# First attention of three fused transformer layers: when VectorE normalises the heads, and in which order TensorE and ScalarE take the neighbouring work

## The reference, cut to what matters

```
h = layer_norm(x, ln1_g, ln1_b)
q, k, v = split(h @ w_qkv.T)              # 16 heads of 16 features
scores = q_chunk . [k_previous_chunk, k_chunk] / 4      # chunks of 128 tokens
valid: the 128 keys that end with the query's own       # j >= i+1 and j <= i+128
attn = softmax(scores, -1);  out = attn @ [v_previous, v_chunk]
x = x + out @ w_o.T
x = x + mlp(layer_norm(x, ln2_g, ln2_b))  # 256 -> 1024 -> 256, gelu
```

## Time and profile before

| | |
|---|---|
| median of 3 runs | 1760.74 us |
| profiled execution, its own time | 1759.69 us |
| its span in the trace | 1757.9 us |
| granted TensorE clock, mean | 0.996 |
| PE busy / DVE / ACT / POOL | 1695.5 / 1446.6 / 1170.4 / 1052.0 us |
| reciprocals of attention A (one per chunk) | 32, from 40.0 to 371.2 us |

### The profile page before, as it was taken

The page is one execution under the profiler, slowest core; times in us unless marked ns, Lnnn a source line. Parts: engine busy times, 40 slices in busy tenths (PEclk is TensorE's granted clock), DMA queues, the critical chain, the costliest instruction groups (busy, mean ns, idle before and its releaser), DMA issues.

```text
span 1757.9 us, 43282 instructions
## 1 busy us (share of the span) xinstructions
PE 1695.5 (96%) x15168; PEld 1460.7 (83%) x15168; DVE 1446.6 (82%) x3686; ACT 1170.4 (67%) x3024; POOL 1052.0 (60%) x1052
## 2 busy tenths in 40 slices
PE   6999999989999999999998999999999999999997
PEld 4777777779998788888887888878888888888886
DVE  6888988868887999989997655579999999967776
ACT  6999888855544778878775343367787787743332
POOL 3676566534334687887774444367878777634333
PEclk9999999999999999999999999999999999999999
DMA  3111211022322322222223313122222222131221
GB/s 109 38 38 38 65 38 35 26 103 66 117 72 65 98 81 66 76 76 66 80 67 89 107 54 99 54 92 75 80 63 81 72 70 81 56 111 60 73 84 37
DMA packets 174626, 125.44 MB, mean 71 GB/s; under 512 B 20824, under 2 KB 173664, under 8 KB 173664
## 3 DMA queue, kind: packets, MB, share of 16 engines
q1 hardware_dynamic: 174432, 122.98, 23.0%
HBM read 88.32 MB, written 34.61 MB: 70 GB/s over the span
## 4 chain that ended last, share of the span: by engine, by line
PE 84%; DVE 9%; ACT 3%; issue 3%; DMA 1%; POOL 0%; SPq 0%; POOLq 0%; DVEq 0%; ACTq 0%
PE psum L612 18%; PE psum L614 17%; PE psum L613 17%; PE psum L948 6%; PE psum L916 5%; PE psum L929 5%; PE psum L727 3%; PE psum L709 3%; PE psum L890 3%; ACT a_probs L1757 2%; PE psum L662 1%; DVE a_neg_max L1240 1%; DVE psum L1238 1%; PE psum L699 1%; PE psum L1053 1%
## 5 line engine op out<-in xcount | busy, mean ns | idle before, releaser
L1876 ACT ACTIVATE b_probs<-masked,neg_max 128x256 f32<-128x256 f32 (+1 forms) x512 | 249.8, 489 | 119.4 <-DVE neg_max L1370 119.4
L612 PE MATMUL psum<-wa_hi,b_h_hi 128*128 128x512 f32 (+1 forms) x576 | 234.4, 407 | 6.0 <-DVE wa_lo L1167 3.6
L614 PE MATMUL psum<-wa_hi,b_h_lo 128*128 128x512 f32 (+1 forms) x576 | 214.1, 372 | 0.0
L613 PE MATMUL psum<-wa_lo,b_h_hi 128*128 128x512 f32 (+1 forms) x576 | 214.0, 372 | 0.0
L1370 DVE CUSTOM_DVE_ANT_0 masked<-psum,mask 128x256 f32<-128x256 f32 (+1 forms) x512 | 177.2, 412 | 41.1 <-PE psum L916 40.2
L612 PE MATMUL psum<-g_h_hi,wm_hi 128*128 128x512 f32 (+1 forms) x480 | 190.3, 397 | 3.5 <-POOL g_h_lo L2148 2.4
L2105 POOL TENSOR_TENSOR g_in<-g_in,minus_half 128x16 f32<-128x16 f32 x64 | 187.7, 2933 | 5.3
L614 PE MATMUL psum<-g_h_hi,wm_lo 128*128 128x512 f32 (+1 forms) x480 | 189.2, 394 | 0.0
L613 PE MATMUL psum<-g_h_lo,wm_hi 128*128 128x512 f32 (+1 forms) x480 | 189.2, 394 | 0.0
L1962 ACT ACTIVATE gate<-psum,vec_b 128x512 f32<-128x512 f32 x96 | 66.0, 687 | 153.6 <-PE psum L614 153.5
L612 PE MATMUL psum<-wm_hi,u_hi 128*128 128x256 f32 x576 | 164.5, 286 | 0.1
(11 more groups left out here) (167 smaller groups left out, 5432.6 us busy)
## 6 DMA issues: line engine op xcount, KB each, us to landing
b_inv_t<-inverse_rows SPq DMA_DIRECT2D x128, 128.0 KB, 3.0
x_mid<-y_out SPq DMA_DIRECT2D x96, 128.0 KB, 2.3
rope_in<-in_rope SPq DMA_DIRECT2D x64, 128.0 KB, 2.4
x_res<-x_state SPq DMA_DIRECT2D x64, 128.0 KB, 2.8
g_in<-x_mid SPq DMA_DIRECT2D x32, 256.0 KB, 3.7
w_raw<-in_w_mlp_b SPq DMA_DIRECT2D x2, 2154.0 KB, 9.1
x_in<-in_x SPq DMA_DIRECT2D x32, 128.0 KB, 2.2
x_res<-in_x SPq DMA_DIRECT2D x32, 128.0 KB, 2.2
```

The costliest lines, as they stand in the source:

```text
L612: nc.tensor.matmul(out, a_hi, b_hi, start=first, stop=False)
L613: nc.tensor.matmul(out, a_hi, b_lo, start=False, stop=False)
L614: return nc.tensor.matmul(out, a_lo, b_hi, start=False, stop=last)
L1876: ins = nc.scalar.activation(out, src, ACT.Exp, bias=neg_max[:, r, k:k + 1], scale=-1.0, accum_out=row_sum[:, n % 2, 4 * r + k:4 * r + k + 1])
```

## The change

Three orders are changed; no instruction is added or removed.

- VectorE: `normalize_heads` is split into `invert_heads` (the reciprocal, still first) and `normalize_heads` (the multiplication), which now comes behind `maxima(4s)` and ahead of `maxima(4s+1)`.
- TensorE: `project_qk(s+1)` moves ahead of `transpose_o(s-2)` and `transpose_z(s+2)`.
- ScalarE: `o_high(s-2)` moves behind `exponentials(4s)`.

```diff
@@ TensorE, pe_attention_a
                 if a_chunk(s - 1):
                     transpose_probs(4 * s - 1)
-                if a_chunk(s - 2) and s < NCH - 1:
-                    transpose_o(s - 2)
                 if s == NCH - 1:
...
                     pe_mlp(pe, MLP_A, MA, None, opening="z")
-                if s == -1:
-                    project_qk(0)
+                if a_chunk(s + 1):
+                    project_qk(s + 1)
+                if a_chunk(s - 2) and s < NCH - 1:
+                    transpose_o(s - 2)
                 if a_chunk(s + 2):
                     transpose_z(s + 2)
-                if a_chunk(s + 1) and s > -1:
-                    project_qk(s + 1)
                 if a_chunk(s):
                     transpose_probs(4 * s)
@@ VectorE, dve_attention_a
-            def normalize_heads(n):
+            def invert_heads(n):
                 v.wait_ge(S["out_steps"], a_out_step(n, 0))
                 src = bank[a_heads_bank(n)].rearrange("p (h d) -> p h d", d=32)
                 nc.vector.reciprocal(a_inv[:], src[:, :, 16]).then_inc(S["o_ready"], 1)
+
+            def normalize_heads(n):
+                src = bank[a_heads_bank(n)].rearrange("p (h d) -> p h d", d=32)
                 v.wait_ge(S["o_ready"], 2 * n + 1)
...
                 if a_chunk(s - 2) and s != NCH + 1:
+                    invert_heads(s - 2)
+                if a_chunk(s):
+                    maxima(4 * s)
+                if a_chunk(s - 2) and s != NCH + 1:
                     normalize_heads(s - 2)
                 if a_chunk(s):
-                    maxima(4 * s)
                     maxima(4 * s + 1)
...
                 elif s == NCH:
+                    invert_heads(NCH - 1)
                     normalize_heads(NCH - 1)
@@ ScalarE, act_attention_a
+                if a_chunk(s):
+                    exponentials(4 * s)
                 if a_chunk(s - 2) and s != NCH - 1:
                     o_high(s - 2)
-                if a_chunk(s):
-                    exponentials(4 * s)
                 if a_chunk(s + 1):
                     copy_twice(s + 1, 1)
```

## The result

The changed kernel takes 1772.15 us (median of 6 runs, 1766.77 to 1772.75) against 1760.58 us (6 runs, 1759.04 to 1761.61). By the medians it is slower by 11.6 us, where 6.1 us were forecast. The ratio estimated from the runs is 1.0054, with a 95% interval of 1.0043 to 1.0065; that is 9.5 us (7.6 to 11.4), less than the medians say. The six runs of the changed kernel lie at two levels, two at 1766.77 and 1768.62 us and four from 1772.07 to 1772.75. The median lies 0.65 us above the upper end of the forecast's range (1771.5). The sign and the path of the delay held; one term of the sum was too small, and about 2.5 us of the median lie outside the steps (an estimated 1.2 of them the clock in step 31).

The account below looks back on a forecast made before the run. TensorE, busy for 96%, was taken as the bound. 27 steps at 0.20 us (5.4) plus 0.28 (step 17), 0.33 (step 29) and 0.1 us (step 31) made 6.1 us, giving 1766.8 us, range 1759.5 to 1771.5.

Parts of the forecast that it names:

- the path of the delay: Second scores, heads, first scores, first maximum, first exponentials, `o_high`, k, second exponentials, second scores: 0.20 us shifts the whole step.
- First maximum: VectorE: moving the multiplication gains the step's first maximum 0.00 us, since the scores hold it.
- faster: Rival: the multiplication holds the first maximum, so 29 steps give back 8.4 us, 1752.3 us; chance 0.14.
- `o_high`'s place: ScalarE, between first exponentials and the copy of k: 0.28 us less 0.08 us of slack, 0.20 us a step.
- `transpose_o` "just in time": TensorE: the multiplication releases `transpose_o` at 214.88, it could begin near 214.89; `o_high` released at 215.54, when ScalarE reaches it.
- larger loss: Rival: VectorE's whole 0.33 us slip reaches the second scores in every step, 9.6 us, 1770.3 us; chance 0.12.
- the second maximum: VectorE: moves back by 0.33 us, to an end at 216.15, and no longer matters to the second exponentials.
- The range's lower end: Lower end of the forecast's own range, 1764.5 to 1769.5 us, given as 0.15 to 0.3 us a step.
- step 17: Fewer values matmuls and no slack before its second scores, so it loses 0.28 us.
- step 29: VectorE also carries the MLP's statistics and ScalarE waits for its maximum, so the full 0.33 us counts.
- Step 31: No `o_high` there; MLP transposes wait for heads about 1.7 us later, filling a 1.23 us gap: about 0.1 us.
- The gap: TensorE's idle before the transposes of a step's first probabilities, held by ScalarE's exponentials, stays at 0.29 us.

Follow-up runs that it names:

- gates by part: Kernel before, with each of a round's four transposes waiting for its own exponential instead of all four: 1759.55 us against 1762.80, ratio 0.9982.
- ScalarE's edit alone: Kernel before with only `o_high` moved behind the exponentials of round 4s: 1768.17 us, ratio 1.0027.
- without VectorE's: Changed kernel with the multiplication back before the step's first maximum, TensorE's and ScalarE's edits kept: 1766.93 us, ratio 1.0031.
- VectorE's edit alone: Kernel before with only the split of reciprocal and multiplication on VectorE: 1802.56 us against 1762.14, one run.
- the second trace: Changed kernel timed again with no edit: 1771.78 us against 1762.80, ratio 1.0050.
- trace 3: Changed kernel again with no edit, first of three more traces: 1769.58 us, one run, against 1763.44 for the kernel before.
- the first trace: Profiled execution of the changed kernel's first measurement, the fastest of its six runs: 1766.77 us.
- the changed kernel's gates by part: Changed kernel with each transpose of probabilities waiting for its own exponential: 1769.93 us against 1762.14, ratio 1.0047.
- the two with `o_high` in its old place: Kernel before with VectorE's edit alone, 1802.56 us, and with TensorE's and VectorE's edits, 1800.89 us, against 1762.14.

## Why the prediction was right, and where it was too small

**First maximum.** Forecast 0.00 us, measured 0.00 (0.69 behind the reciprocal in both). The chain named the multiplication, which stood just ahead on VectorE, although the scores came 0.06 us later; so small a gap is not marked. The rival "faster" is out. The Trainium skill, "Perfetto Trace Analysis", section "Optimization Strategy", says to find the gaps of the engine that counts and to make what they wait for start sooner. The kernel with gates by part agrees with it (1.6 us in the stage): it acts on what released those transposes. The change acted on something that was not late.

**`o_high`'s place.** Forecast 0.20 us a step, measured 0.20 (ScalarE's edit alone), 0.19 (without VectorE's) and 0.20 in step 30 of the changed kernel. An estimate from the figures of the Trainium skill, "ScalarE: Activation LUTs", section "What ACT_TABLE_LOAD costs", has the instruction hand on after 0.31 us; the runs show 0.26 to 0.28, and these decide.

**`transpose_o` "just in time".** This is the term that was mis-sized. I let the multiplication release `transpose_o` 0.01 us ahead of what TensorE could take, priced that at zero, and let `transpose_z` start 0.22 us later and release `o_high` 0.43 us after that. Two prices were wrong. Where the weights are not loaded ahead the first distance is 0.28 us, and `transpose_z` starts 2.77 us behind the reciprocal instead of 2.73. And from `transpose_z` to an `o_high` that waits for it are 0.48 us, in VectorE's edit alone (237.55 to 238.03), where the wait is marked, and as much in the changed kernel (230.26 to 230.74), where it is too short to be marked. That makes 0.09 us: `o_high` at 3.25, not 3.16, where ScalarE alone would let it start at 3.17. Measured 0.08 us a step against the kernel without VectorE's edit, 2.0 us over 27 steps. The rival "larger loss" had named this meeting point, with 0.33 us a step in all; the measured 0.27 lies halfway between its size and the forecast's 0.20. Of its mechanism one half is out: the second maximum ended 3.77 us behind the reciprocal, as forecast, and held nothing. The other half happened, smaller than priced: `transpose_z`, behind the late `transpose_o`, held `o_high`.

The working has a slip beside this. The projection was given 1.45 us, but its own rows give 215.05 + 0.23 - 213.80 = 1.48, so `transpose_o` would have come at 214.92. In the changed kernel the projection does take 1.48 us; but it starts 0.98 us behind the reciprocal, not 1.06 as assumed, so TensorE was free a little earlier than forecast and the multiplication released `transpose_o` at 2.49 (forecast 2.51). The two errors nearly cancel, by luck. The range's lower end has a smaller slip: 0.15 us in 29 steps makes 1765.1, not 1764.5.

**Single steps.** The rest of the stage, 8.9 - 6.0 - 2.0 = 0.9 us, is spread: step 17 took 0.38 more (forecast 0.28) and step 29 0.36 (0.33); above the typical 11.06 were step 2 (0.14; 0.06 in the second trace, none in trace 3), step 7 (0.27), step 8 (0.14, in the first trace alone) and steps 18, 23 and 28 (0.10 to 0.12). In step 7 ScalarE idles ahead of `o_high` for no other instruction:

```profile
97.94 0.39 ACT L1784 ACTIVATE b_h_hi<-psum 128x256 fp32r<-128x256 f32 x1 [0.24 <-issue]
```

Step 7 is long in all five traces and in the one without VectorE's edit (11.21), and not in ScalarE's edit alone. With the changed kernel's gates by part it is long as well (11.32). What holds the issue there, and `transpose_z` by 0.1 us in steps 18, 23 and 28, was not tested.

**Step 31.** Forecast 0.1, measured 0.2, and 1.2 to 1.3 more where the clock falls. The MLP's transposes now wait for the heads:

```profile
363.97 0.52 PE L1051 MATMUL psum<-ident,g_z 128*128 128x128 f32 x3 [1.47 <-DVE mask L1248]
```

**The gap.** TensorE's idle before the first transposes was to stay near 0.29 us. It is 0.28 where the multiplication is early and 0.19 in step 19 of the changed kernel (5.8 us over 27 waits), since `transpose_o` and `transpose_z` start later; the transposes themselves still start 3.34 us behind the reciprocal.

**The sum.** In the profiled executions: 8.9 us in the stage, 0.2 in step 31, 1.0 less at the start and 1.1 less in the rest, that is 7.0 us, against 6.1 forecast. That this execution took 1766.77 us, the forecast to 0.03, is luck: the steps alone cost 9.1 us, and 2.1 came back outside them for other reasons. In the medians: 11.6 us, of which 9.1 are the steps and an estimated 1.2 the clock in step 31 (three traces of five have it); 1.3 are open. Whether the change makes that fall more frequent isn't settled. With the gate as before, four of seven traces with the late multiplication have it (three of five of the changed kernel, one of the two with `o_high` in its old place), and none of the four with the early one. The idle times of TensorE are 1.47 and 1.9 us in the first group and 1.24 and 1.9 in the second; so few traces can't tell.

## What to carry to other kernels

A chain names one instruction at each step, not by how much it beat the next condition, and it can name the wrong one of two that lie a few hundredths of a us apart. Before an instruction is moved off it, read from the timelines when each other condition was met, and price the move at the smaller of the two. When a moved instruction now arrives "just in time" for a transpose, don't price that at zero: look for a row in which the weights are not loaded ahead and use its distance. And measure a change of a few us by a distance inside the trace that repeats between traces (here 29 steps, to 0.6 us), since the whole span moved by 3 us for other reasons.

## What the runs showed of the hardware

- A pair of transposes whose weight load waited for the operand came 0.28 us ahead of the next pair (changed kernel, 229.98 to 230.26), against 0.22 us (before) and 0.21 us (without VectorE's edit) where the load ran ahead: 0.06 to 0.07 us more.
- A ScalarE instruction that waited for a pair of transposes started 0.48 us behind the start of the pair (VectorE's edit alone), which is 0.10 us behind the end that its row gives it (0.38 us).
- The granted clock fell to 0.5 for some 3 us after one and the same idle of 1.90 us in three of five executions of one program, and made the four transposes behind it take up to 1.11 instead of 0.66 us.
- Such short falls came at a handful of places. One between 573 and 627 us is in all thirteen traces; those near 24, 372, 950 and 1545 us are in some traces of the changed kernel and not in others.
